# Loop's end: one shared product ahead of the last probabilities, the shared layers' banks exchanged, the experts' numbers read sooner

## What is computed

```
logits = xf @ gate_w.T;  one expert of 8 per token (top_k, K = 1, weight 1)
y  = w2[e] @ (silu(w1[e] @ x) * (w3[e] @ x))
y += gelu(x @ sw1.T) @ sw2.T
```

## Time and profile before

| | us |
|---|---|
| runs, median of 3 | 650.7 (650.46 to 653.05) |
| profiled execution, its own time | 652.26 |
| its span | 650.3 |
| PE busy | 633.1 (97%) |
| DVE busy | 405.8 (62%) |
| POOL busy | 321.2 (49%) |
| ACT busy | 304.1 (47%) |
| mean granted clock of PE | 0.997 |

### The profile page before, as it was taken

The page is one execution under the profiler, slowest core; times in us unless marked ns, Lnnn a source line. Parts: engine busy times, 40 slices in busy tenths (PEclk is TensorE's granted clock), DMA queues, the critical chain, the costliest instruction groups (busy, mean ns, idle before and its releaser), DMA issues.

```text
span 650.3 us, 14315 instructions
## 1 busy us (share of the span) xinstructions
PE 633.1 (97%) x4237; PEld 531.2 (82%) x4239; DVE 405.8 (62%) x1033; ACT 304.1 (47%) x719; POOL 321.2 (49%) x336
## 2 busy tenths in 40 slices
PE   5979999999999999999999999999989999999998
PEld 3867888887888888788888778877769999999997
DVE  7876666666666665666666666777565455455540
ACT  3325444455454455444455544444573534443433
POOL 2355544455554455454445454444875315555551
PEclk9999999999999999999999999999999999999999
DMA  8521343343543343343343334111255623333232
GB/s 302 219 97 34 90 105 81 94 115 83 113 109 86 85 117 89 81 100 94 81 109 102 81 91 104 38 37 41 65 143 176 193 54 44 47 47 44 43 38 66
DMA packets 72262, 60.77 MB, mean 93 GB/s; under 512 B 6832, under 2 KB 60976, under 8 KB 71856
## 3 DMA queue, kind: packets, MB, share of 16 engines
q1 hardware_dynamic: 65600, 56.26, 31.9%
q0 software_dynamic: 6640, 4.22, 4.7%
HBM read 17.31 MB, written 26.82 MB: 68 GB/s over the span
## 4 chain that ended last, share of the span: by engine, by line
issue 32%; PE 31%; POOL 27%; DVE 6%; POOLq 2%; ACT 1%; DMA 0%; SPq 0%; ACTq 0%; DVEq 0%
PE bank L1292 29%; POOL z L497 6%; POOL e3l L492 5%; POOL g L486 4%; POOL e L479 4%; POOL z L499 3%; POOL rstd L506 3%; PE bank L1635 1%; DVE z L955 1%; POOL z L501 1%; POOLq L479 1%; PE bank L1471 0%; POOLq L505 0%; DVE ident_b L1128 0%; DMA h<-x_prev 0%
## 5 line engine op out<-in xcount | busy, mean ns | idle before, releaser
L1292 PE MATMUL bank<-whigh,uth 128*128 128x512 f32 x512 | 170.0, 412 | 1.2 <-DVE lowt L849 1.2
L1292 PEld LDWEIGHTS bank<-whigh,uth 128*128 128x128 f32 x512 | 89.6, 189 | 25.9 <-issue 7.4
L1292 PE MATMUL bank<-whigh,utl 128*128 128x512 f32 x256 | 101.2, 395 | 0.0
L585 POOL DMA_INDIRECT out<-prob,ids x39 | 60.9, 1561 | 66.8 <-ACT prob L803 66.8
L497 POOL TENSOR_TENSOR z<-z 128x512 f32<-128x512 f32 x32 | 42.6, 1332 | 100.4 <-DVE z L955 100.4
L506 POOL TENSOR_TENSOR rstd<-rstd,powers 128x1 f32<-128x1 f32 x64 | 35.2, 551 | 101.7 <-DVE rstd L942 55.0
L1292 PE MATMUL bank<-xvo,x 128*128 128x128 f32 x624 | 76.3, 275 | 0.0
L1292 PEld LDWEIGHTS bank<-xvo,x 128*128 128x128 f32 x624 | 72.8, 192 | 0.2 <-issue 0.2
L955 DVE TENSOR_TENSOR z<-bank,v 128x512 f32<-128x512 f32 x64 | 44.2, 691 | 31.6 <-PE bank L1292 27.8
L1292 PE MATMUL bank<-xT,qkw 128*128 128x128 f32 x512 | 62.5, 275 | 0.0
L1292 PEld LDWEIGHTS bank<-xT,qkw 128*128 128x128 f32 x512 | 59.8, 192 | 0.4 <-ACT xT L619 0.3
(11 more groups left out here) (231 smaller groups left out, 1351.8 us busy)
## 6 DMA issues: line engine op xcount, KB each, us to landing
sorted_rows<-blank SPq DMA_DIRECT2D x24, 709.5 KB, 5.5
xvp<-xvo SPq DMA_DIRECT2D x128, 128.0 KB, 2.3
w<-w_t SPq DMA_DIRECT2D x1, 4096.0 KB, 12.1
xvo<-sorted_rows SPq DMA_DIRECT2D x39, 64.5 KB, 1.8
out<-h SPq DMA_DIRECT2D x9, 256.0 KB, 3.3
w<-w_high SPq DMA_DIRECT2D x4, 512.0 KB, 6.4
x_columns<-x2t SPq DMA_DIRECT2D x32, 64.0 KB, 1.6
xg_in<-x_columns SPq DMA_DIRECT2D x8, 256.0 KB, 4.9
```

Source lines behind the costliest of these rows:

```text
L585: nc.gpsimd.indirect_dma_start(out=out[:, :], out_offset=bass.IndirectOffsetOnAxis(ap=ids[:, j:j + 1], axis=0), in_=y[:, 2 if j == SORTED ...
L1292: return T.matmul(out_, lhsT, rhs, start=start, stop=stop)
```

## The change

- `UP_BANKS`: group 1's `up` and gelus use banks 0, 5, 1, 2 for chunks 0 to 3. `down_bank`: groups 0 and 1 use banks 6 and 5 for `down` and the sum, later groups 5 and 6 as before.
- In `last_two` on PE, chunk 1 of group 1 and `router(29)` now stand ahead of `prob_columns(31)`; chunks 2 and 3 of group 1 follow it, with waits for gelus 2 and 3 of group 0. Chunk 0 of group 2 takes the place that chunk 3 of group 1 had, ahead of `router(31)`. The other three chunks of group 2 follow behind a wait for all gelus of groups 0 and 1.
- `down(2, 0)` waits for `added` 2 (the sums of groups 0 and 1).
- ACT: gelu 1 of group 1 stands ahead of the x2 copy of tile 30.
- DVE: the loop over groups 2 to 5 is written out, as its banks are no longer a matter of `k` alone.
- PE: the wait for the experts' numbers and the reading of the first two stand between `up(5, 1)` and `down(4, 0)`.

```diff
@@ -74,6 +74,7 @@
 CHOOSE_STEPS, ROUTE_STEPS = 5, 2 * 14 + 1 + 8
 CHOOSE_AT, RANK_AT, PLACE_AT, SCATTER_AT = EARLY + 1, EARLY + 2, EARLY + 3, EARLY + 4
 SMALL_STEPS, NORM_STEPS = 21, 9
+UP_BANKS = ((0, 1, 2, 3), (0, 5, 1, 2))
 LAST_CHUNKS = (1, 3, 0, 2)
 LAST_UP_BANKS = ((3, 4, 1, 2), (0, 7, 3, 4))
 PRODUCT_STEP, OUT_COLUMN_STEP, SUMS_STEP, SQUARED_STEP = 1, 3, 4, 5
@@ -87,6 +88,11 @@
 def is_tile(i, t):
 
     return isinstance(i, int) and i == t
+
+
+def down_bank(g, k):
+
+    return 6 - k if g < 2 else 5 + k
 
 
 def build(nc, x_next, x_prev, w_low, w_high, tok_b, wqkv, u_qkv, wout_t, u_columns, b_out,
@@ -710,9 +716,9 @@
                 keep_logits(LAST_BUT_ONE - 1, 4)
                 gelus(0, 0, range(3, HC))
                 gelus(1, 1, range(1))
+                gelus(1, 1, range(1, 2))
                 x2_transposed(LAST_BUT_ONE, False, 4)
                 keep_x2(LAST_BUT_ONE)
-                gelus(1, 1, range(1, 2))
                 keep_logits(LAST_BUT_ONE, 4)
                 x_group_hi(2, 0)
                 x2_transposed(LAST, False, 4)
@@ -769,7 +775,8 @@
             def gelus(g, k, chunks=range(HC)):
                 for c in chunks:
                     a.wait_ge(up_psum, g * HC + (c + 1))
-                    A.activation(gelu[k][c], B[c][:], ACT.Gelu).then_inc(gelu_done, 1)
+                    bank = UP_BANKS[1][c] if is_tile(g, 1) else c
+                    A.activation(gelu[k][c], B[bank][:], ACT.Gelu).then_inc(gelu_done, 1)
 
             iteration(TILES - 3, False, True)
             a.wait_ge(y_psum, 2 * TILES)
@@ -1193,7 +1200,7 @@
             def add_shared(g, k):
                 d.wait_ge(down_psum, g + 1)
                 hg = h[:, bass.ds(g * GROUP, GROUP), :].rearrange("p t d -> p (t d)")
-                V.tensor_tensor(hg, hg, B[5 + k][:], ALU.add).then_inc(added, 1)
+                V.tensor_tensor(hg, hg, B[down_bank(g, k)][:], ALU.add).then_inc(added, 1)
 
 
             d.wait_ge(lg_sb, TILES)
@@ -1222,7 +1229,7 @@
             V.tensor_copy(row_i[:], row_f[:]).then_inc(pos_ready, 1)
             assert n_route == ROUTE_STEPS
 
-            with d.Fori(2, GROUPS - 3, 2) as g:
+            for g in range(2, GROUPS - 3, 2):
                 for k in range(2):
                     x_group_lo(g + (k + 2), k)
                     add_shared(g + (k - 1), 1 - k)
@@ -1416,16 +1423,16 @@
                 for c in chunks:
                     if not first:
                         pe.wait_ge(gelu_done, g * HC + (c + 1 - HC))
-                    three(B[c][:], [sw1[:, n, col(c)] for n in range(2)], (xgh[k], xgl[k])) \
-                        .then_inc(up_psum, 1)
+                    three(B[UP_BANKS[1][c] if g == 1 else c][:], [sw1[:, n, col(c)] for n in range(2)],
+                          (xgh[k], xgl[k])).then_inc(up_psum, 1)
 
             def down(g, k, tiles=range(GROUP), first=False):
                 pe.wait_ge(gelu_done, (g + 1) * HC)
                 if not first:
-                    pe.wait_ge(added, g - 1)
+                    pe.wait_ge(added, 2 if g == 2 else g - 1)
                 for t in tiles:
                     for c in range(HC):
-                        last = mm(B[5 + k][:, col(t)], gelu[k][c][:, col(t)], sw2[:, c, :],
+                        last = mm(B[down_bank(g, k)][:, col(t)], gelu[k][c][:, col(t)], sw2[:, c, :],
                                   c == 0, c == HC - 1)
                 if GROUP - 1 in tiles:
                     last.then_inc(down_psum, 1)
@@ -1547,12 +1554,17 @@
                 values(LAST_BUT_ONE)
                 up(0, 0, range(3, HC), True)
                 pe.wait_ge(pT_sb, LAST)
-                up(1, 1, range(1))
+                up(1, 1, range(1), True)
                 pe.wait_ge(shifted, TILES)
                 x2_columns(LAST_BUT_ONE - 1, 4)
+                pe.wait_ge(vo_sb, 2 * TILES)
+                up(1, 1, range(1, 2), True)
+                router(LAST_BUT_ONE - 1, 4)
                 prob_columns(LAST)
-                router(LAST_BUT_ONE - 1, 4)
-                up(1, 1, range(1, 3))
+                pe.wait_ge(gelu_done, 2)
+                up(1, 1, range(2, 3), True)
+                pe.wait_ge(gelu_done, 3)
+                up(1, 1, range(3, HC), True)
                 pe.wait_ge(h2_done, LAST)
                 values(LAST)
                 down(0, 0, range(1), True)
@@ -1563,7 +1575,7 @@
                 down(0, 0, range(3, GROUP), True)
                 pe.wait_ge(lg_sb, LAST)
                 x2_columns(LAST, 4)
-                up(1, 1, range(HC - 1, HC))
+                up(2, 0, range(1))
                 router(LAST, 4)
 
             sum_level2(0)
@@ -1614,7 +1626,8 @@
                 iteration(i, True, True, True)
             iteration(TILES - 3, False, True, True)
             last_two()
-            up(2, 0)
+            pe.wait_ge(gelu_done, 2 * HC)
+            up(2, 0, range(1, HC))
             pe.wait_ge(route, 14 + CHOOSE_STEPS)
             pe.wait_ge(lg_sb, TILES)
             mm(B[4][:, 0:rest * EXPERTS], below, oh.rearrange("p t e -> p (t e)"))
@@ -1671,13 +1684,13 @@
                 last.then_inc(ed_psum, 1)
 
             up(AHEAD - 1, 1)
+            pe.wait_ge(pos_ready, 3)
+            e = {0: expert(0), 1: expert(1)}
             down(AHEAD - 2, 0)
-            pe.wait_ge(pos_ready, 3)
             pe.wait_ge(ld_w2, 16)
             pe.wait_ge(gelu_done, AHEAD * HC)
             rows_in_columns(0, 0, True)
             rows_in_columns(1, 1, True)
-            e = {0: expert(0), 1: expert(1)}
             down(AHEAD - 1, 1, range(2))
             expert_up(0, 0, True)
             down(AHEAD - 1, 1, range(2, GROUP))
```

## The result

The changed kernel takes 655.85 us (median of 17 runs, 653.1 to 657.75); the kernel before, run beside it, 650.46 (17 runs, 649.19 to 653.09). The ratio is 1.0075, 95% interval 1.006 to 1.009: slower, by 5.4 us in the medians. The profiled execution shown here is one of 655.85 us, with a span of 653.9.

A forecast was written before the change was run, and what follows sets the result against it. The prediction took TensorE (PE) to bound the kernel, busy 633.1 of 650.3 us. Its terms: 652.26 - 1.7 + 1.2 + 2.9 + 1.4 - 0.5 = 655.56, say 655.6 us; range 653.3 to 657.3.

The forecast's parts named there:

- The banks exchanged: At down(2, 0): PE waits for group 1's sum, made behind the routing on DVE; +2.9 us, other bound 3.5.
- the prediction's remark: At down(2, 0): both times count from the rank products, so an earlier or later loop's end changes nothing.
- Clock behind the wait: Behind the wait at down(2, 0): PE runs at 1.2 GHz for a stretch; +1.4 us, bounds 0 and 1.7.
- the prediction's two rows: Before's trace: 1.28 and 0.25 us idle, then 1.2 GHz; 1.97 us idle in the preparation, then 2.4 GHz.
- Loop's end: In last_two on PE: +0.5 us up to the value products, +0.7 behind them; together +1.2, bounds 0 and 1.6.
- The usual run has no half clock at loop's end: At loop's end: the profiled 652.26 us has a half-clock stretch costing 1.7 that the usual run lacks; -1.7.
- Reading: Ahead of the last down(5, 1): reading the experts' numbers sooner hides it; -0.5 us, bounds 0 and -0.59.
- The written-out loop on DVE: DVE's loop written out adds no operation and DVE waits for PE there; costed at nothing.
- Rival 1: Behind the wait at down(2, 0): the clock stays up, 654.2 us; chance 0.2.
- Rival 2: At loop's end: the half-clock stretch comes in most executions of the changed kernel too, 657.3 us; chance 0.15.
- Rival 3: At down(2, 0): group 1's sum is already made, so not slower; 651.3 us, or 650.1; chance 0.06.
- rival 4: Between up(5, 1) and down(4, 0): the reading still stalls, 656.1 us; no chance of its own, inside the forecast's range.

The follow-up runs named there:

- banks exchanged alone: The kernel before with only the down banks of groups 0 and 1 exchanged and the wait for group 1's sum: 657.02 us, ratio 1.0102.
- the filled wait: The changed kernel with 11 products of a constant put between up(3, 1) and down(2, 0), the wait for group 1's sum kept: 654.39 us, ratio 1.0061.
- reading alone: The kernel before with only the reading of the first two experts' numbers moved ahead of down(4, 0): 650.4 against 650.71 us, ratio 0.9994.
- DVE's loop written out: The kernel before with the experts' numbers read sooner and VectorE's loop over groups 2 to 5 written out: 650.31 us, ratio 0.9995.

## Why the prediction was right, step by step

- **The banks exchanged** (+2.9): 507.81 against 504.93, 6.99 us behind the rank products, where it starts without this wait: 2.9. The sum ended 9.7 us behind the rank products, predicted 9.9. Both experiments that take the cause away remove it. The reason for the lower bound, that group 4's load stands earlier against the rank products in the changed kernel, is shown by "banks exchanged alone", where it does not, and where the wait was 4.0 (507.31 against 503.35), beyond the prediction's upper bound of 3.5. So loop's end does change something here, against the prediction's remark: the sum ended 9.7 us behind the rank products with one order and 10.8 with the other.
- **Clock behind the wait** (+1.4, bounds 0 and 1.7): 3.4 us at 0.52. From the rank products to the row transposes it is 27.81 us where before had 23.31, 4.5 more, of which the wait is 2.9: the clock costs 1.6. That it comes from standing still was argued, and is now shown by the filled wait. The argument for its size, by the length of the gap, was weak, and that it held was in part luck. Of the prediction's two rows, the shorter idle time (1.28 and 0.25) was the costly one, and its brackets were followed by half clock in only two of four traces. Another row of the same trace, not used, speaks against it: the wait of 3.95 us with which PE's timeline of before begins is followed by full clock. Timeline and windows view:

```profile
3.95 1.19 PE L1292 MATMUL bank<-v,sq 128*128 128x256 f32 x2 [3.95 <-DVE v L863]
```

```profile
3.95:7.35 3.40, 2.16 (x3) 0.97 (x4) 2.28 (x6) 0.00 (x0) 0.00 (x0) 1.00 0.95 297
```

  What PE did ahead of that first wait is in no trace, so it may be a case of its own; what decides between the two levels stays open. The Trainium skill ("TensorE: Matmul & The Clock Gate", section "HAM oscillation — how this bites in real kernels") tells of waits of about 3 to 5 us between bursts, behind which the next burst begins slow, at a cost of half of the throttled time. The cost agrees here: half of 3.4 us is 1.7, measured 1.6. The wait of 2.71 us is shorter than those it tells of, and the clock fell all the same. So are the idle times of 1.28 and 1.97 us by which the prediction judged it, so that it says nothing of them by itself.
- **Loop's end** (+1.2): +1.5, from 16.5 undisturbed to 18.0. Mechanism and brackets were right (1.1, 0.6, 0.5 and 0.9 as differences of starts), the size was short in both parts. Up to the value products it is 0.6 us (8.26 from the last scores, 7.67 in "reading alone"), predicted 0.5: the router behind its wait takes 0.25 (485.25 to 485.50) where 0.14 was taken. Behind them it is 0.9, predicted 0.7: the `three` behind its wait takes 0.81 (493.89 to 494.70) where 0.7 was taken, and 0.74 was rounded down. The gelu moved up on ACT cost nothing, as assumed: ACT stood idle for 1.73 us ahead of the next x2 copy (490.52). By the two partial experiments the router's place is worth 0.6 in this stage and chunk 0's place with its waits 1.0.
- **The usual run has no half clock at loop's end**: the assumption that let the sum go against the median. Of four profiled executions with before's loop's end, the one shown ahead of the prediction and "DVE's loop written out" have it (18.1 us), the other two don't (16.5). No trace of the median run exists, so that it lacks the stretch is not shown. Nor is it the only thing in which executions differ. The mean granted clock of every run beside the experiments is known: of 81 runs of before, 48 have 0.995, about two stretches like this one (each takes some 0.0026 off the mean, an estimate: half of 3.4 us in 650), 14 have 0.997 and 12 have 1.0, and their mean times are 650.8, 650.9 and 651.2 us. In nine of the twelve traces stretches at half clock stand in the preparation, between 13 and 41 us, and eight of these nine reach loop's end no later (478.4 to 479.8 us) than the three without (479.8 to 479.9). So taking the price of one stretch off one execution, to get the usual run, met the median within 0.1 us partly by luck.
- **Reading** (-0.5): alone 0.46. The written-out loop on DVE, costed at nothing, gives 0.3 more, as the first copy of weights starts sooner: that term was wrong, and small. Together 0.78.

With the measured terms: 650.5 + 1.5 + 2.9 + 1.6 - 0.8 = 655.7, measured 655.85; predicted 655.6. Loop's end was 0.3 short and the clock 0.2, and the gain was 0.3 short too, so that the errors cancel in part: the sum is closer than its terms.

Rival 1 (clock stays up) is out for the changed kernel's profiled execution, though five of the 17 runs, 653.1 to 653.8, lie near where it would put them. Rival 2's second stretch may stand behind the slow runs: the six with a mean granted clock of 0.994 or less have a mean time of 656.7, the eleven others 654.9. Where a run's stretches stood, its mean clock does not say, so neither is settled for the runs without a trace. Rival 3 fell with the bracket at `down(2, 0)`, rival 4 with "reading alone", where nothing stalls at the new place.

## What to carry to other kernels

Before giving a buffer to another group, look at who frees it and what stands ahead of the freeing instruction in that engine's order: here a 0.7 us sum stood behind 4 us of routing, and moving that sum ahead of the routing in DVE's order took the whole wait away. A gap filled on the engine that bounds the kernel is worth only what the next wait lets through; write down for each moved product which release comes last now. A wait on TensorE costs its length and may cost more behind it: here 2.9 us of waiting and 1.6 us of clock. And where idle time hangs on a chain through other engines, measure the stage up to the next fixed point, not the bracket alone: 1.0 us gained at loop's end was 0.2 us at the row transposes.

## What was not expected of the hardware

- The granted clock at loop's end differs between executions with the same brackets (1.28 and 0.25 or 0.26): 0.91 over the stage in two, 1.00 in two.
- PE's first wait, 3.95 us in the trace of before and 5.19 in that of "banks exchanged alone", was followed by 3.4 us at 1.00 in both, while the waits of 2.71 and 3.82 us ahead of `down(2, 0)` were followed by 1.2 GHz.
- A wait of 3.8 us was followed by twice as long a stretch at 1.2 GHz (0.51 from 507.0 to 513.6) as one of 2.7 (0.52 from 507.8 to 511.2), so 1.1 us more of waiting cost 2.5 in all from the rank products to the row transposes (30.31 against 27.81).
- Where a loop on DVE was written out, the first copy behind it, which needs a register read, started 0.2 us sooner (bracket 0.40 against 0.60, one trace of each) and the second had no bracket where it had 0.41.
